# Splitting the layer normalisation of the projection stage in halves and moving its statistics

## The reference, cut to what matters

```python
def reference(x, Wq, Wk, Wv, Wo, ...):            # x: (16, 1024, 256)
    x = x + layernorm(attn(layernorm(x)))          # differential attention
    x = x + layernorm(ffn(layernorm(x)))           # tokens chosen per expert
    return x

def layernorm(x, eps=1e-5):
    return (x - mean(x)) / sqrt(var(x) + eps)      # over the last 256 values

def attn(x):                                       # its head, which the change touches
    q, k, v = x @ Wq, x @ Wk, x @ Wv
    q, k = rope(q) * scaling, rope(k)              # pairs (q0, q1) are rotated by cos and sin
    ...
```

## Time and profile before

| what | us |
|---|---|
| median of 3 runs | 5975.78 |
| lowest and highest | 5975.41 and 5980.85 |
| the profiled execution: its own time | 5969.97 |
| the profiled execution: span | 5968.1 |
| GpSimd's first and last operation of the projections | 0.24 and 453.1 (end) |

### The profile page before, as it was taken

One profiled execution on the slowest core, in us unless ns is written; L12 is line 12 of the kernel. 1 busy time (PEld: TensorE's weight loads), 2 busy tenths in 40 slices (PEclk: granted clock), 3 DMA queues, 4 the chain that ended last, 5 costly groups with the idle time before them and its releaser, 6 DMA issues. The chain is left out here.

```text
span 5968.1 us, 167678 instructions
## 1 busy us (share of the span) xinstructions
PE 5593.6 (94%) x50896; PEld 1978.1 (33%) x50896; DVE 5489.2 (92%) x6110; ACT 4965.0 (83%) x9174; POOL 2070.4 (35%) x3560
## 2 busy tenths in 40 slices
PE   8878999999999999999999999999999999987776
PEld 4542333333333333333333333333333333325524
DVE  7868999999999999999999999999999999966716
ACT  6665999999999999999999999999999999983313
POOL 7981222222222222222222222222222222235506
PEclk9997999999999999999999999999999999998878
DMA  5671222232222222222232222222222222206587
GB/s 181 204 209 46 52 53 53 53 52 53 52 53 52 53 51 51 52 51 51 50 52 53 53 53 53 52 53 51 53 53 53 53 50 52 50 15 202 198 341 309
DMA packets 408166, 495.27 MB, mean 83 GB/s; under 512 B 132051, under 2 KB 265331, under 8 KB 395235
## 3 DMA queue, kind: packets, MB, share of 16 engines
q1 hardware_dynamic: 406499, 485.74, 32.5%
q10 hardware_dynamic: 1024, 0.53, 0.0%
HBM read 360.60 MB, written 123.21 MB: 81 GB/s over the span
## 5 line engine op out<-in xcount | busy, mean ns | idle before, releaser
L741 DVE TENSOR_REDUCE at_largest<-at_ps_m 128x1 f32<-128x1024 f32 x4096 | 4695.6, 1210 | 43.2 <-PE at_ps_m L845 28.7
L707 ACT ACTIVATE at_e<-at_ps_e 128x512 f32<-128x512 f32 x8192 | 4409.6, 598 | 351.8 <-PE at_ps_e L814 153.3
L831 PE MATMUL at_ps_o<-at_e,at_v 128*32 128x256 f32 (+1 forms) x30720 | 2680.3, 421 | 31.3 <-ACT at_e L707 20.6
L845 PE MATMUL at_ps_m<-k_stack,q_stack 48*128 48x512 bf16 x8192 | 2484.3, 384 | 87.8 <-DVE at_largest L741 55.6
L814 PE MATMUL at_ps_e<-q_stack,k_stack 51*128 51x512 bf16 x8192 | 2514.6, 382 | 8.4 <-issue 2.1
L831 PEld LDWEIGHTS at_ps_o<-at_e,at_v 128*32 128x32 f32 x30720 | 844.9, 149 | 1556.5 <-issue 818.0
L814 PEld LDWEIGHTS at_ps_e<-q_stack,k_stack 51*128 51x128 bf16 x8192 | 567.7, 93 | 1665.4 <-ACT at_e L707 1632.5
L626 POOL TENSOR_TENSOR at_negated<-at_zeros,at_largest_t 128x32 f32<-128x32 f32 x256 | 64.9, 254 | 2165.3 <-DVE at_largest_t L748 2165.3
L845 PEld LDWEIGHTS at_ps_m<-k_stack,q_stack 48*128 48x128 bf16 x8192 | 573.8, 93 | 219.8 <-DVE at_largest L741 188.2
L669 POOL TENSOR_TENSOR at_rms<-at_mean_eps,at_minus_half 128x16 f32<-128x16 f32 x128 | 372.8, 2912 | 10.0
L645 POOL TENSOR_TENSOR at_crossed<-at_totals 128x32 f32<-128x32 f32 x128 | 32.4, 253 | 750.8 <-DMA at_totals<-at_sums 750.8
(11 more groups left out here) (130 smaller groups left out, 3005.6 us busy)
## 6 DMA issues: line engine op xcount, KB each, us to landing
k_stack<-k_parts SPq DMA_DIRECT2D x1536, 64.0 KB
q_stack<-q_parts SPq DMA_DIRECT2D x256, 192.0 KB
q_stack<-q_parts SPq DMA_DIRECT2D x256, 128.0 KB
w_first<-in_w SPq DMA_DIRECT2D x32, 1024.0 KB, 23.4
ex_w_second<-in_w SPq DMA_DIRECT2D x32, 1024.0 KB, 26.1
q_parts<-pr_parts SPq DMA_DIRECT2D x96, 256.0 KB, 2.5
k_parts<-pr_parts SPq DMA_DIRECT2D x96, 256.0 KB, 2.8
pr_x_in<-in_x SPq DMA_DIRECT2D x16, 1024.0 KB, 5.7
```

The lines of the kernel that those rows point to most:

```text
L707: nc.scalar.activation(e[:, j % E_BUFS], ps_e[:, bank(u, j)], ACT.Exp, scale=SCALE).then_inc(exp_done, 1)
L741: nc.vector.reduce_max(largest[:, u % 2, j // SIDE, j % SIDE:j % SIDE + 1], ps_m[:, j % 2], AX.X).then_inc(max_done, 1)
L831: last = nc.tensor.matmul(ps_o[32 * tile:32 * tile + 32, columns], v[:, u, tile // 2, first:first + 2 * VD * TILES - kt:TILES], e[:, (QUAD ...
L845: last = nc.tensor.matmul(ps_m[:, j % 2, half * HALF:(half + 1) * HALF], q_stack[rows, u, pair, c, t * P:(t + 1) * P], k_stack[rows, u, pa ...
```

## The change

1. `normalise` is made in halves of four tiles. `normalise(n + 1, half 0)` opens ScalarE's slot 0 and half 1 opens slot 1; before, all eight stood at the end of slot 0. `xn_ready` counts halves.
2. The four copies of transposed input are made in pairs that open slots 2 and 3; before, all four opened slot 3. TensorE's transposes of banks 0 and 1 wait for half 0 alone, banks 2 and 3 for half 1.
3. GpSimd's `scale` shrinks from four operations to two, the power and one multiplication. VectorE makes the other two at the end of `statistics`: minus the mean, and variance plus eps, as two `tensor_scalar` on 128x8 values, behind a wait for `bn_aggr`.
4. `statistics(n + 2)` stands at the end of VectorE's slot 1 instead of slot 2. `scale(n + 2)` stays in GpSimd's slot 3.

```diff
                 def scale(m):
                     pool.wait_ge(var_done, m + 1)
-                    nc.gpsimd.tensor_tensor(var[:], mean_var[:, :, 1], eps[:], ALU.add).then_inc(pool_step, 1)
-                    pool.wait_ge(pool_step, 3 * m + 1)
                     if not (isinstance(m, int) and m == 0):
-                        pool.wait_ge(xn_ready, m)
+                        pool.sem_inc(pool_passed, 1)
+                        pool.wait_ge(xn_ready, 2 * m)
                     nc.gpsimd.tensor_tensor(rstd[:], var[:], minus_half[:], ALU.pow).then_inc(pool_step, 1)
-                    pool.wait_ge(pool_step, 3 * m + 2)
-                    nc.gpsimd.tensor_tensor(shift[:], mean_var[:, :, 0], rstd[:], ALU.mult).then_inc(pool_step, 1)
-                    pool.wait_ge(pool_step, 3 * m + 3)
-                    nc.gpsimd.tensor_tensor(bias[:], zeros[:], shift[:], ALU.subtract).then_inc(rstd_done, 1)
+                    pool.wait_ge(pool_step, m + 1)
+                    nc.gpsimd.tensor_tensor(bias[:], neg_mean[:], rstd[:], ALU.mult).then_inc(rstd_done, 1)
...
-                def normalise(m, u):
+                def normalise(m, u, side):
                     act.wait_ge(rstd_done, m + 1)
                     if not (isinstance(m, int) and m == 0):
-                        act.wait_ge(t_done, TILES // 2 * m)
-                    for t in range(TILES):
+                        act.wait_ge(t_done, KC * (2 * m - 1 + side))
+                    for t in range(side * TILES // 2, (side + 1) * TILES // 2):
...
                 def slot(n, i, u, ch, has, more, more2):
-                    if ch == 3 and more:
-                        for j in range(4):
+                    if ch < 2 and more:
+                        normalise(n + 1, 1 - u, ch)
+                    if ch >= 2 and more:
+                        for j in range(2 * (ch - 2), 2 * (ch - 1)):
                             copy_transposed(n + 1, 1 - u, j)
...
-                    if ch == 0 and more:
-                        normalise(n + 1, 1 - u)
...
                     for t in range(TILES):
                         last = nc.vector.bn_aggr(mean_var[:, t], stats[:, t])
-                    last.then_inc(var_done, 1)
+                    last.then_inc(dve_step, 1)
+                    dve.wait_ge(dve_step, 2 * m + 2)
+                    nc.vector.tensor_scalar(neg_mean[:], mean_var[:, :, 0], -1.0, None, ALU.mult)
+                    nc.vector.tensor_scalar(var[:], mean_var[:, :, 1], EPS, None, ALU.add).then_inc(var_done, 1)
...
-                    if ch == 2 and more2:
+                    if ch == 1 and more2:
                         statistics(n + 2, i + 1, u)
...
                 def transposes(m, banks):
-                    pe.wait_ge(xn_ready, m + 1)
                     for j in banks:
+                        if j % KC == 0:
+                            pe.wait_ge(xn_ready, 2 * m + j // KC + 1)
```

More of the change, by code:

```diff
@@ L125, in project @@
             w = sb("w", [P, KC, 3, D])
-            eps, minus_half, zeros = sb("eps", [P, TILES]), sb("minus_half", [P, TILES]), sb("zeros", [P, TILES])
+            minus_half = sb("minus_half", [P, TILES])
             x_in = sb("x_in", [P, 2, TILES, D])
@@ L129, in project @@
             var, rstd = sb("var", [P, TILES]), sb("rstd", [P, TILES])
-            shift, bias = sb("shift", [P, TILES]), sb("bias", [P, TILES])
+            neg_mean, bias = sb("neg_mean", [P, TILES]), sb("bias", [P, TILES])
             xn = sb("xn", [P, TILES, D])
@@ L151, in project @@
             v_stored = [sem("v_stored0"), sem("v_stored1")]
-            dve_step, pool_step, passed = sem("dve_step"), sem("pool_step"), sem("passed")
+            dve_step, pool_step, passed, pool_passed = sem("dve_step"), sem("pool_step"), sem("passed"), sem("pool_passed")
             x = io["x"].rearrange("b (t p) d -> b p t d", p=P)
@@ L202, in load @@
                 def load(n, u):
-                    sp.wait_ge(xn_ready, n - 1)
+                    sp.wait_ge(xn_ready, 2 * (n - 1))
                     sp.dma_start(x_in[:, u], x[bass.ds(n, 1)].rearrange("o p t d -> (o p) t d")).then_inc(x_loaded[u], 16)
@@ L240, in _ @@
             def _(pool):
-                nc.gpsimd.memset(eps[:], EPS).then_inc(pool_set, 1)
                 nc.gpsimd.memset(minus_half[:], -0.5).then_inc(pool_set, 1)
-                nc.gpsimd.memset(zeros[:], 0.0).then_inc(pool_set, 1)
                 nc.gpsimd.memset(ones[:], 1.0).then_inc(ones_set, 1)
-                pool.wait_ge(pool_set, 3)
+                pool.wait_ge(pool_set, 1)
                 pool.wait_ge(ones_set, 1)
@@ L350, in drain @@
                     second_part(c - 1, (c - 1) % RING)
-                normalise(0, 0)
+                for side in range(2):
+                    normalise(0, 0, side)
                 for j in range(4):
@@ L370, in statistics @@
                     last.then_inc(dve_step, 1)
-                    dve.wait_ge(dve_step, m + 1)
+                    dve.wait_ge(dve_step, 2 * m + 1)
                     if not (isinstance(m, int) and m == 0):
```

## The result

The changed kernel takes **5943.86 us** in the median of five runs (5943.42 to 5947.59). The kernel before, run beside it five times, takes 5977.04 (5975.41 to 5981.66). The ratio is 0.9944, with a 95% interval of 0.9930 to 0.9957: faster by 0.56%, 33 us between the medians. The profiled execution of the changed kernel took 5943.86 (span 5942.0), that of the kernel before 5969.97, so between the two profiles the difference is 26.1.

What follows compares the result with a forecast made beforehand. The prediction took a loop through GpSimd, with its wait for `bn_aggr`, as the bound. 20.0 (wait) + 7.8 (`scale`) + 1.1 (start) - 4.1 (end) = 24.8 us; 5975.8 - 24.8 = 5951.0, range 5945 to 5958, with rivals 5946 to 5987.

Steps and rivals of the forecast that it cites:

- GpSimd's cycle of 23.71 us: GpSimd's loop per batch after the change, taken as the pace: 25.81 - 1.54 - 0.56 = 23.71 us.
- the copy chain: Last steps before the next batch's q: `leave_out` of slot 0, `second_part`, copy of v, copies of banks 2 and 3.
- The wait of 1.54: GpSimd's wait for `bn_aggr` ahead of `scale`; expected to go 13 times, 20.0 us.
- The two `tensor_scalar`: On VectorE: the first waits for a GpSimd operation, the second slips in by 0.04 to 0.07 us.
- R2: Rival: both `tensor_scalar` wait for GpSimd; 26.8 us per batch, 5986 us, slower; chance 0.28.
- The second close meeting: VectorE's `leave_out` of slot 0 and GpSimd's next `third_part` reach the port 0.04 us apart; first, `leave_out` ends at T + 3.5.
- T: The end of the GpSimd `third_part` that runs ahead of VectorE's pair of `tensor_scalar`.
- R1: Rival: `leave_out` loses the second close meeting, the copy chain becomes the loop; 25.2 us per batch, 5967 us; chance 0.24.
- the term of 1.1: Start of the projections: TensorE's first transposes follow half a normalisation; 1.1 us gained.
- 4.1 given back: Last four batches: a faster pace meets stores that have not landed; half of 4 x 2.1, 4.1 us lost.
- R3: Rival: the small `tensor_scalar` on VectorE don't wait at all; 5948 us; chance 0.04.
- R4: Rival: the 1.54 us gap only moves elsewhere, the pace stays and only the start gains; 5975 us; chance 0.06.

Runs made afterwards that it cites:

- the operations behind: Changed kernel plus two small `bn_aggr` (extra work) on VectorE behind the second `tensor_scalar`: 5990.6 us, one run, 5.6 over the kernel before.
- them between: Changed kernel plus two small `bn_aggr` (extra work) on VectorE between the two `tensor_scalar`: 5982.2 us, one run, 2.8 under the kernel before.
- the old places: Changed kernel with both halves of `normalise` back at the end of slot 0 and all four copies heading slot 3: 5990.8 us, one run.

## Why the prediction was wrong, and what it had right

The direction held, and so did what the two moves do and how both port meetings go. The number did not: 5943.9 is 7.1 us under the forecast of 5951.0 and 2 us below the lower end of the range. Two steps failed. The sum took GpSimd's cycle of 23.71 us as the pace of a batch, where the copy chain sets it and a batch takes 23.27. And a difference worked out on one profile was put on the median of the runs unchanged; that alone is 5.8 of the 7.1 us. The sum itself missed the difference of the two profiles, 26.1, by only 1.3, but by errors that nearly cancel: 5.5 too little in twelve batches, 1.6 too much at the start, 0.6 at the end, and 2.1 in the other stages. That it came so close is luck.

**What bounded the kernel before: right.** With statistics in slot 2 the gain is gone (5974.8), so the wait for `bn_aggr` is on the path. That the halves and the pairs of copies are needed as well, or TensorE would still need 25.81, was right too: with statistics alone TensorE waits for the copies and nothing is gained, and with the halves alone GpSimd's wait of 1.5 stays.

**The wait of 1.54: right.** `bn_aggr` ends at 223.06 and the power operation starts at 229.38, some 6 us later, without a wait. In the whole stage three such waits are left, 15.1 us, where the earlier trace rows had sixteen with 39.1:

```profile
POOL pr_rstd L253 <- DVE pr_var L376: 15.1, 3, 8.6
```

**The two `tensor_scalar`: right, and as thin as said.** 0.81 us in the median for the first, 0.157 for the second. 0.16 us more between them turns 0.157 into 2.25. The Trainium skill, page "SBUF — State Buffer", section "Who interferes with whom", lets the engine that issues first have the shared ports. The trace agrees for these two: the second one gets in because it asks before the next `add`, and the rule gave R2 only by taking the queued operation as issued.

**The second close meeting: right.** `leave_out` was put at T + 2.25 and is at T + 2.29 (226.21 with T = 223.92), and it wins. With 0.16 us of delay it loses and ends at T + 5.5, as R1 has it.

**GpSimd's cycle of 23.71: the term that was mis-sized.** The measured period is 23.27, and over twelve batches that is 12 x 2.56 = 30.7 us, against 12 x 2.10 = 25.2 of the 27.8 in the sum (the rest stood for the last batches). The 1.06 us of `bias` were carried over as GpSimd's own work. They were 0.20 of work and 0.86 of waiting for `leave_out`, which started 0.22 ahead of it. The row to read was the `shift` operation above it: the same shape, 0.20. In the changed kernel `leave_out` runs under the power operation, and `bias` takes 0.20. Against that the gap ahead of `add` grew from 0.34 to about 0.72: 23.71 - 0.86 + 0.38 = 23.23. The gap grew because the bound moved. GpSimd, with 22.44 us of work, now waits for TensorE, and TensorE for the copies.

**The copy chain was the bound, and the prediction had its length.** R1's sum gives 25.2 with `leave_out` ending at T + 5.5; the winning case ends at T + 3.5, so 25.2 - 2.0 = 23.2. The measured period is 23.27, and with the copies moved up it becomes 22.90. The prediction worked out the chain for the rival alone and took GpSimd's 23.71 for the forecast, where both loops should have been summed for each case. "TensorE should wait about 1 us per batch ahead of q": it waits 0.6, in the place named.

**Start and end: mixed, and small.** The start was to gain 1.1. Batch 1 comes 0.5 later in the profile of the changed kernel, because its first q group is long and that of the kernel before isn't. In the second profile of the changed kernel it isn't either, and the first v group starts at 22.69 (24.62 in the kernel before, 25.20 in the first profile):

```profile
19.55 5.81 PE L436 MATMUL pr_ps_q<-pr_xn_t,pr_w 128*128 128x512 f32 x8 [0.68 <-ACT pr_xn_t L311]
```

```profile
19.15 3.70 PE L436 MATMUL pr_ps_q<-pr_xn_t,pr_w 128*128 128x512 f32 x8 [0.67 <-ACT pr_xn_t L311]
```

The kernel before shows both forms as well. Like with like, q of batch 1 starts 2.1 us earlier where the first group is short (41.77 against 43.90) and 1.8 where it is long (44.29 against 46.04), so the term of 1.1 was about 1 us too small.

Behind batch 13 the sum had 27.8 - 25.2 = 2.6 of gain and 4.1 given back, 1.5 lost in all. The gain is 30.3 at batch 13 and 28.2 at the start of the next stage, so 2.1 were lost, and 3.7 between the second profiles of the two kernels (35.0 and 31.3), by the mechanism named: ScalarE stands for stores of q parts.

```profile
348.39 1.04 ACT L317 CAST pr_parts<-pr_rotated 128x1024 bf16<-128x1024 f32 x1 [12.11 <-DMA q_parts<-pr_parts]
```

From profile to profile the projections gain 28.2, and the other stages take 2.1 us more. In fourteen profiles of this case, the two of either kernel included, these stages take 5502.7 to 5514.8 us, so that is their own spread.

**Putting the difference on the median: the step that cost most.** The sum of 24.8 compares with 26.1 between the profiles, and 5945.2 with 5943.86, within 1.3. But the profile of the kernel before lay 7.1 below the median of its runs, that of the changed one on its median. Of the 68 timed runs of the kernel before on record, 5971.0 to 5991.8, none is as short as the profiled 5969.97. The start of the next stage moved by 6.7 us between two profiles of that kernel. One profile against its median holds such a spread, and the range should have been widened downward by it; its lower end of 5946 stood only 5 under the forecast. Between medians the change gains 33.2 us here and 39.4 in the later comparison (5985.0 and 5945.6), between the two pairs of profiles 26.1 and 27.7 (spans). What the kernel before does in the rest of that time no profile on record shows.

**The rivals.** R1 and R2 are real mechanisms, each lying within 0.16 us of timing of the changed kernel, but neither has the price that was given. R1 was foretold at 25.2 per batch and 9 us faster than before. The kernel that loses the second meeting takes 26.96 in most batches and is 5.6 us slower than before, as far as one run can tell. Missing was the clock: 1.7 us in most batches, behind a TensorE wait of 2.6, which the prediction even gave, as 2.8. So R1 should have lent nothing to "faster", where it had lent a third of its chance. R2 was foretold at 26.8, and 27.17 was measured, but by two errors that nearly cancel. `leave_out` doesn't wait for the power operation: it ends at T + 5.74 (T = 220.42, the end of `third_part` in that batch), not at T + 7.1. So the chain alone is 26.8 - 1.36 = 25.44, and with the clock's 1.70 it is 27.14. Both kernels, made on purpose and run once each, came out within 0.1% of the kernel before. R3 and R4 are out: the first `tensor_scalar` waits, and the batch is 2.56 us shorter. What the prediction called thin was thin: the gain hangs on two meetings of a few hundredths of a microsecond.

## What to carry to other kernels

Before a forecast, sum every loop that could set the pace for every case, and take for each small operation the shortest row of its shape as its work; the rest is waiting that can vanish or come back. When a change or a rival leaves TensorE a longer wait, price the clock behind it too: here 1.7 us behind a wait of 2.6, as much as the waits under dispute, though only where TensorE's chain sets the pace. A difference read from one profile is not the difference of medians; take the spread between executions into the range. A gain that rests on who reaches a port first should be tried with a small delay on either side, and parts that gain nothing alone may gain together.

## What the runs showed of the hardware

**Longer work on TensorE can shorten the loop.** In the steady batches (batches 2 to 13), no group behind a wait of 1.4 to 1.8 us was slow in the kernel before or in the one with `scale` on GpSimd. Behind 2.0 to 2.2 us some were (5 of 8 with statistics in slot 2, 4 of 7 with halves alone), behind 2.6 to 2.9 most (9 of 12 with the operations behind, and 10 of 12 each with them between, with the old places and with statistics alone). A slow group of q takes 5.4 us instead of 3.7, at a granted clock of 0.50. It costs 1.7 us where the copy chain sets the pace. Where GpSimd's wait for `bn_aggr` sets it (statistics in slot 2, halves alone) it costs nothing. With 3.44 us of matmuls in the wait no group was slow, and a batch took 25.83 instead of 26.96 or 27.17.

**A running power operation does not hold up VectorE.** `leave_out` (two inputs in SBUF, 1.21 us) starts 0.22 behind the 1.65 us power operation on 128x8 in all twelve steady batches of the changed kernel, and neither is longer than alone. The other way round, with `leave_out` running first, the power operation takes 2.58 to 2.62 and a 0.20 us product 1.06. The same section of the Trainium skill says that a VectorE instruction with two SBUF inputs contends with a GpSimd instruction that reads SBUF; the trace agrees where VectorE is first and shows no such contention where the small power operation is.

**The first matmuls of the program may be long.** The first q group takes 5.8 or 5.9 us in one profile and 3.7 in another of the same kernel, in both kernels. In the long one of the changed kernel the matmuls start about 0.85 us apart up to 23.1 and 0.43 from 23.9 on, which is the ratio of TensorE's two clock levels. The clock itself is not on record there before 23.8, and what decides between the two forms was not tried.
